# Attention of a small vision tower: values held still and turned probabilities streamed, instead of the other way round

## The reference, cut to what matters

```python
q, k, v = ...                                  # (64, 16, 37, 16), q and k rotated
scores = einsum('bhtd,bhsd->bhts', q, k) / sqrt(16)
probs = softmax(scores, axis=-1)
attn = einsum('bhts,bhsd->bhtd', probs, v)
attn = attn.transpose(0, 2, 1, 3).reshape(B, T, C)
h = h + attn @ Wout + bout
```

## Time and profile before

| | us |
|---|---|
| median of three executions | 336.23 |
| the profiled execution | 335.01 |
| its span in the trace | 333.2 |
| PE busy in the span | 304.5 (91%) |
| DVE busy | 254.3 (76%) |
| ACT busy | 195.0 (59%) |
| POOL busy | 138.9 (42%) |

### The profile page before, as it was taken

One profiled execution on the slowest core, in us unless ns is written; L12 is line 12 of the kernel. 1 busy time (PEld: TensorE's weight loads), 2 busy tenths in 40 slices (PEclk: granted clock), 3 DMA queues, 4 the chain that ended last, 5 costly groups with the idle time before them and its releaser, 6 DMA issues.

```text
span 333.2 us, 9403 instructions
## 1 busy us (share of the span) xinstructions
PE 304.5 (91%) x3575; PEld 232.7 (70%) x3583; DVE 254.3 (76%) x666; ACT 195.0 (59%) x366; POOL 138.9 (42%) x262
## 2 busy tenths in 40 slices
PE   8989899999999977998999999999768999999784
PEld 8877676777777644656877777877645777776552
DVE  1778996677757774356888877887489999999982
ACT  0323433545544335447655666655548999999992
POOL 0356665645654467437900000000065565666520
PEclk9999999999999999999999999999999999999996
DMA  6799560010000100113211121111000001000011
GB/s 227 230 369 401 165 223 17 18 36 17 19 17 17 36 17 17 51 35 79 54 42 44 40 47 45 40 47 29 3 0 0 3 32 34 31 33 31 33 48 55
DMA packets 19307, 22.38 MB, mean 67 GB/s; under 512 B 2304, under 2 KB 15888, under 8 KB 19264
## 3 DMA queue, kind: packets, MB, share of 16 engines
q1 hardware_dynamic: 18544, 20.89, 19.3%
q10 hardware_dynamic: 720, 0.90, 1.0%
HBM read 16.76 MB, written 5.02 MB: 65 GB/s over the span
## 4 chain that ended last, share of the span: by engine, by line
PE 68%; DVE 18%; ACT 8%; issue 4%; POOL 1%; DVEq 0%; ACTq 0%
PE ps L414 15%; PE ps L454 10%; PE ps L528 9%; DVE sc L913 7%; PE ps L551 7%; PE ps L432 5%; DVE ximg L934 4%; PE ps L518 4%; PE ps L402 4%; PE ps L536 3%; ACT ximg L1125 3%; PE ps L462 2%; ACT ximg L1120 2%; PE ps L499 2%; PE ps L393 2%
## 5 line engine op out<-in xcount | busy, mean ns | idle before, releaser
L1159 POOL TENSOR_TENSOR rs<-rs,nhalf 128x1 f32<-128x1 f32 (+1 forms) x76 | 45.4, 597 | 159.2 <-DVE rs L907 101.2
L414 PE MATMUL ps<-w_in,xT 128*128 128x256 f32 (+1 forms) x228 | 52.6, 380 | 0.6 <-ACT xT L992 0.6
L414 PEld LDWEIGHTS ps<-w_in,xT 128*128 128x128 f32 (+1 forms) x228 | 41.2, 187 | 6.5 <-ACT xT L992 0.8
L1077 ACT ACTIVATE ximg<-ps 128x296 f32<-128x296 f32 x64 | 26.6, 418 | 30.0 <-PE ps L528 29.4
L998 ACT ACTIVATE hn<-h,nmr,rs 128x256 f32<-128x256 f32 (+1 forms) x19 | 11.4, 600 | 54.9 <-POOL nmr L1179 54.9
L454 PE MATMUL ps<-w_qk,hnT 128*128 128x512 f32 (+1 forms) x76 | 36.2, 598 | 3.5 <-DVE qb L793 3.5
L528 PE MATMUL ps<-tab,ximg 128*128 128x128 f32 x256 | 34.9, 279 | 0.0
L851 DVE TENSOR_REDUCE ximg<-ps 128x16 f32<-128x592 f32 x32 | 24.7, 772 | 13.3 <-PE ps L518 13.1
L1166 POOL TENSOR_TENSOR qa<-qa,qb 128x512 f32<-128x512 f32 (+1 forms) x19 | 24.1, 1266 | 13.0 <-DVE qb L793 13.0
L528 PEld LDWEIGHTS ps<-tab,ximg 128*128 128x128 f32 x256 | 27.4, 141 | 1.3
L714 DVE SCALAR_TENSOR_TENSOR h<-ymid,rs,ps 128x256 f32<-128x256 f32 (+1 forms) x19 | 9.1, 480 | 24.8 <-PE ps L393 20.4
(11 more groups left out here) (110 smaller groups left out, 666.6 us busy)
## 6 DMA issues: line engine op xcount, KB each, us to landing
ximg<-in_x SPq DMA_DIRECT2D x18, 384.0 KB, 10.3
ximg<-vsc SPq DMA_DIRECT2D x64, 51.0 KB, 1.9
vsc<-vt SPq DMA_DIRECT2D x18, 136.0 KB, 1.7
out<-ximg SPq DMA_DIRECT2D x18, 128.0 KB, 1.7
ximg<-in_W SPq DMA_DIRECT2D x2, 1024.0 KB, 6.3
qkT<-in_W SPq DMA_DIRECT2D x2, 384.0 KB, 4.8
wide<-in_rows SPq DMA_DIRECT2D x1, 640.0 KB, 10.5
qkT<-in_offsets ACTq DMA_DIRECT2D x1, 512.0 KB, 4.0
```

Source lines behind the costliest of these rows:

```text
L414: mm = pe.matmul(dst[0:n, :], xT[t % 2][:, k, 0:n], w_in[:, k, :], start=(k == 0), stop=(k == KP - 1))
L1077: act.activation(pT[p % 2][:, g0:g0 + 4, :, :], ps_pT(b), ACT.Copy).then_inc(S[f"p_evac{b}"], 1)
L1159: pool.tensor_tensor(rs[u][0:n, i:i + 1], rs[u][0:n, i:i + 1], nhalf[0:n, :], ALU.pow).then_inc(S[done], 1)
```

## The change

The roles in `attend` are exchanged. A pair of heads' 32 value columns are held still and the turned probabilities of one image (37 columns) stream. The output comes out turned: 32 features on 32 partitions (32c to 32c+31, c = 0 to 3), tokens along the free dimension. The column of ones is gone; instead four matmuls a pair of images hold a block of ones (`head_sum`, 128 x 32: the first 16 columns sum the even head's rows, the last 16 the odd head's) and stream 148 columns each, which gives the sum of each token and head repeated on that head's 16 partitions. `normalise` now takes a reciprocal of 128 x 148 and multiplies 128 x 148 straight into the canvas. `turn_out` and `attended_out` go, with the semaphores o_norm, o_turned and a_init and the two memsets of PSUM on DVE (L880, L884). The value row in `vt`, `vsc` and `vb` grows from 272 to 512 numbers: each head pair takes 32 columns, with zeros where the other head's values would be, set once by POOL.

```diff
-VROW = 2 * HC * VW
+VROW = 2 * D
...
+        head_sum = sb("head_sum", [128, 2, HD])
...
-                    src = bass.AP(vsc.tensor, PW * p * VROW + e * HC * VW,
-                                  [[VROW, 48], [TOK * VROW, 2], [1, HC * VW]])
-                    sp.dma_start(vb[p % 4][64 * e:64 * e + 48, :, e, :], src).then_inc(S[f"vb{p % 4}"], 16)
+                    src = bass.AP(vsc.tensor, PW * p * VROW + e * D,
+                                  [[VROW, 48], [TOK * VROW, 2], [1, D]])
+                    sp.dma_start(vb[p % 4][64 * e:64 * e + 48, :, :], src).then_inc(S[f"vb{p % 4}"], 16)
...
             def attend(p):
                 war(pe, "o_canvas", p)
-                if p < 2:
-                    pe.wait_ge(S["a_init"], p + 1)
+                if p == 0:
+                    pe.wait_ge(S["qk_rot"], NT + 1)
+                if p == 1:
+                    pe.wait_ge(S["qk_canvas"], NT + 1)
                 pe.wait_ge(S["p_evac4"], p + 1)
                 pe.wait_ge(S["p_evac5"], p + 1)
+                for c in range(4):
+                    probs = pT[p % 2][:, :, :, :].rearrange("p (m c) i t -> p c m (i t)", c=4)[:, c, :, :]
+                    pe.matmul(ps_sums(p % 2)[32 * c:32 * c + 32, :, :], head_sum[:, :, :].rearrange("p e c -> p (e c)"), probs, start=True, stop=True)
                 pe.wait_ge(S[f"vb{p % 4}"], 32 * (p // 4 + 1))
-                for g in range(HC):
+                for m in range(2):
                     for i in range(2):
-                        rhs = vb[p % 4][:, i, :, VW * g:VW * g + VW]
-                        dst = ps[64 * i:64 * i + TOK, 6 + p % 2, 2 * VW * g:2 * VW * g + 2 * VW]
-                        mm = pe.matmul(dst.rearrange("p (e c) -> p e c", e=2), pT[p % 2][:, g, i, :], rhs,
-                                       start=True, stop=True)
+                        for c in range(4):
+                            g = 4 * m + c
+                            mm = pe.matmul(ps_out(p % 2)[32 * c:32 * c + 32, m, TOK * i:TOK * i + TOK],
+                                           vb[p % 4][:, i, 2 * HD * g:2 * HD * g + 2 * HD], pT[p % 2][:, g, i, :],
+                                           start=True, stop=True)
                 mm.then_inc(S["o_ready"], 1)
...
-                if live(s - 3, NP):
-                    turn_out(s - 3)
...
+            for e in range(2):
+                for c in range(2):
+                    v.memset(head_sum[64 * e:64 * e + 64, c, :], 1.0 if c == e else 0.0)
...
             def normalise(p):
                 u = p % 2
                 v.wait_ge(S["o_ready"], p + 1)
-                v.reciprocal(rec[u][0:SPAN, :].unsqueeze(2), ps_o(u)[:, :, HD:VW]).then_inc(S["o_rec"], 1)
+                v.reciprocal(rec[u], ps_sums(u)).then_inc(S["o_rec"], 1)
                 v.wait_ge(S["o_rec"], p + 1)
-                war(v, "o_turned", p, 4)
-                v.tensor_tensor(at[p % 4][0:SPAN, :].rearrange("p (h c) -> p h c", c=HD), ps_o(u)[:, :, 0:HD],
-                                rec[u][0:SPAN, :].unsqueeze(2).to_broadcast([SPAN, NH, HD]), ALU.mult
-                                ).then_inc(S["o_norm"], 1)
+                v.tensor_tensor(qkT[:, 0:2, PW * p:PW * p + PW], ps_out(u), rec[u], ALU.mult
+                                ).then_inc(S["o_canvas"], 1)
...
-            v.memset(ps[:, 6, 0:NH * VW], 1.0).then_inc(S["a_init"], 1)
...
-            v.memset(ps[:, 7, 0:NH * VW], 1.0).then_inc(S["a_init"], 1)
...
-                if live(s - 3, NP):
-                    attended_out(s - 3)
...
-                        ins = pool.memset(vt[u][:, :, :, :], 1.0)
-                    ins.then_inc(S["v_ones"], 1)
+                        ins = pool.memset(vt[u][:, :, :, :, :], 0.0)
+                    ins.then_inc(S["v_blank"], 1)
```

More of the change, by code:

```diff
@@ L33 @@
 K3 = 3 * TOK
-SPAN = 64 + TOK
 V3 = 3 * TOK
-VW = HD + 1
 HC = NH // 2
-VROW = 2 * HC * VW
+VROW = 2 * D
 LAG = 9
@@ L177, in vit_block @@
         later = carve(pix[:, GPX:NT * PD], 2 * [
-            ([NH, 64], F32), ([HC, 2, TOK], F32), ([NH], F32), ([NH], F32), ([2, 128], BF16), ([D], F32)]
-            + 4 * [([D], F32)] + 4 * [([2, 2, HC * VW], F32)])
+            ([NH, 64], F32), ([HC, 2, TOK], F32), ([NH], F32), ([2, PW], F32), ([2, 128], BF16), ([D], F32)]
+            + 4 * [([2, D], F32)])
         pr, pT, mx, rec, nT, ob = zip(later[:6], later[6:12])
-        at, vb = later[12:16], later[16:20]
+        vb = later[12:16]
         ps = ctx.enter_context(nc.psum_tensor("ps", [128, 8, 512], F32))
@@ L194, in vit_block @@
             "w_abs w_tot w_sc w_rc w_q w_done "
-            "orow v_ready v_evac v_ones v_stored0 v_stored1 v_zero p_zero vb0 vb1 vb2 vb3 "
-            "a_init s_ready s_max s_sub s_exp p_turned4 p_turned5 p_evac4 p_evac5 "
-            "o_ready o_rec o_norm o_turned o_canvas "
+            "orow v_ready v_evac v_blank v_stored0 v_stored1 v_zero p_zero vb0 vb1 vb2 vb3 "
+            "s_ready s_max s_sub s_exp p_turned4 p_turned5 p_evac4 p_evac5 "
+            "o_ready o_rec o_canvas "
             "m_set z_ready r_sum r_stat r_aggr r_var r_rstd r_nmr r_norm r_amax r_xs r_rc r_dsc r_rnd r_bias n_turned "
@@ L225, in vit_block @@
         hnT = [sb(f"hnT{u}", [128, 2, 128]) for u in range(HB)]
-        vt = two("vt", [128, 2, HC, VW])
+        vt = two("vt", [128, 2, HC, 2, HD])
         hn = two("hn", [128, D])
@@ L269, in vit_block, with ps_out, ps_sums @@
         ps_w = ps[:, 2, D:D + 2]
-        O_AT = NH * VW
         def ps_pT(b):
             return bass.AP(ps, 512 * b, [[4096, 128], [128, 4], [64, 2], [1, TOK]])
[L275 to L279, removed]
+        def ps_out(u):
+            return ps[:, 6 + u, 0:2 * PW].rearrange("p (m c) -> p m c", m=2)
+        def ps_sums(u):
+            return ps[:, 6 + u, 2 * PW:4 * PW].rearrange("p (m c) -> p m c", m=2)
         def tiles_of(p):
@@ L326, in store_values @@
                 sp.wait_ge(S["v_evac"], t + 1)
-                sp.dma_start(vsc[128 * t:128 * t + n, :], vt[t % 2][0:n, :, :, :].rearrange("p e g c -> p (e g c)")
+                sp.dma_start(vsc[128 * t:128 * t + n, :], vt[t % 2][0:n, :, :, :, :].rearrange("p e g a c -> p (e g a c)")
                              ).then_inc(S[f"v_stored{t % 2}"], 16)
@@ L878, in _ @@
             patch_step(NT + LAG + 1)
-            v.wait_ge(S["qk_rot"], NT + 1)
-            v.memset(ps[:, 6, 0:NH * VW], 1.0).then_inc(S["a_init"], 1)
             attention_step(1)
             attention_step(2)
-            v.wait_ge(S["qk_canvas"], NT + 1)
-            v.memset(ps[:, 7, 0:NH * VW], 1.0).then_inc(S["a_init"], 1)
             for s in range(3, NP + 3):
@@ L1010, in values_out @@
                 if t < 2:
-                    act.wait_ge(S["v_ones"], 1)
+                    act.wait_ge(S["v_blank"], 1)
                 else:
@@ L1014, in values_out @@
                 n = rows(t)
-                act.activation(vt[t % 2][0:n, :, :, 0:HD],
+                act.activation(bass.AP(vt[t % 2], 0, [[VROW, n], [D + HD, 2], [2 * HD, HC], [1, HD]]),
                                ps_v[0:n, :].rearrange("p (g e d) -> p e g d", e=2, d=HD), ACT.Copy
@@ L1065, in _ @@
                     act.activation(w2t[:, :, :], w2[:, :, :], ACT.Abs, accum_out=wabs[:, 1:2]).then_inc(S["w_abs"], 1)
[L1067 to L1071, removed]
             def probs_out(p, b):
@@ L1216, in _ @@
             for u in range(4):
-                pool.memset(vb[u][:, :, :, :], 0.0).then_inc(S["v_zero"], 1)
+                pool.memset(vb[u][:, :, :], 0.0).then_inc(S["v_zero"], 1)
                 patch_step(NT + 3 + u)
```

## The result

The changed kernel took 340.44 us (median of 11 executions, 338.84 to 341.44), the kernel before 336.23 us (median of 11, 335.27 to 338.11). Ratios leave out slow executions, as 594.69 us (rows widened, first time), 508.97 us (one-column matmuls) and 336.90 us (logarithms on ScalarE). The changed kernel is slower by 1.2%, as forecast (341, range 334 to 347).

The account below looks back on a forecast made before the run. PE bounded the kernel before, DVE close behind; DVE would take over. 28 x (2.81 - 2.65) = +4.5, entrance +0.4, exit -0.3: +4.6 us, median 340.8, say 341; range 336 to 345, stretched to 334 to 347.

Parts of the forecast that it names:

- The reciprocal sets the step: DVE in attention: reciprocal of 148 elements takes 1.04 us, DVE step 2.81 us above PE's 2.21; 28 steps cost +4.5 us.
- the quick reciprocal: Rival, DVE normalise: excess is fixed cost, reciprocal 0.40 us, PE sets the step at 2.36, 327 us; chance 0.09.
- Stride charged at nothing: DVE's old reciprocal reads sums 17 words apart in PSUM; this explains none of its time, so no cost was charged.
- eight passes: Rival, DVE normalise: 8.4 ns an element, reciprocal 1.39 us, step 3.16, 351 us; chance 0.04.
- PE's issue stops fall there too, so I add none: PE in attention: its stops for "issue" fall under normalise's 1.3 us while scores waits, adding nothing to the 2.81 us step.
- Column tiles four abreast: PE's new attend: four column tiles overlap 3.1 of 4, 0.76 us; rival of less overlap, 350 or 373 us, chance 0.05.
- Entrance and exit: Ends of attention: first reciprocal delays maximum 3 by +0.4 us; after the last maximum the residual comes earlier, -0.3 us.
- Elsewhere nothing: Outside the step: larger stores and loads and POOL's longer memset of vt were taken to cost 0 us.

Follow-up runs that it names:

- rows widened, first time: Kernel before with only the value rows widened as in the change (512 numbers stored, 256 a load; nothing reads the added ones): ratio 1.0042.
- one-column matmuls: Changed kernel with 16 matmuls of one bf16 column added to each call of attend, 32 more instructions a step, nothing reads them: 348.23 us, ratio 1.0333.
- logarithms on ScalarE: Changed kernel with reciprocals made on ScalarE as exp(-ln(sum)) and half of attend ahead of a wait, whole computation: 334.35 us, ratio 0.9955.
- the prices: Kernel before with reciprocals of several sizes and a multiplication appended to DVE, pow and multiplication to POOL: the 148-element reciprocal 1.02 us, 6.26 ns an element.
- sums thrice: Changed kernel with the four matmuls of sums issued three times over, same results: 367.98 us, ratio 1.0946.
- wide matmul: Changed kernel with one float32 matmul of 128 rows, 128 x 200 columns, added to each attend, 4 more instructions: 342.75 us, ratio 1.0219.
- no sums either: Changed kernel with the reciprocal replaced by a multiplication and the matmuls of sums left out from the third pair on: 330.73 us, ratio 0.9867.
- no reciprocal: Changed kernel with its 128x148 reciprocal replaced by a multiplication by one, division by the sums left out: 335.38 us, ratio 0.9971.

## Why the prediction was right

- **The reciprocal sets the step: right, and nearly in size.** 1.04 us forecast, 1.07 measured; 6.0 ns an element taken, 6.26 measured. The step from 1 to 16 elements between rows of the kernel before pointed the right way, but it was a thin base: back to back the prices have 158 ns for one and 196 for 16, which would have given 2.5 ns an element and spoken for the quick reciprocal; the 6.26 show from 16 elements up (196, 558, 1021). So the size owes something to luck. DVE's clean step came to 2.83 us against 2.81, and with the reciprocal replaced by a multiplication the mean step falls to 2.68 and the time by 5 us.
- **Stride charged at nothing, eight passes rejected: right,** shown by the prices, with the reserve on the stride said there.
- **"PE's issue stops fall there too, so I add none": wrong in size.** The mean step is 2.89, not 2.83: 28 x 0.06 = 1.7 us. A stop is covered only while PE would wait anyway; the one ahead of the row at 163.58 falls into the middle of scores, and the next maximum starts 2.98 us behind the last (160.88 to 163.86) instead of 2.83. Between the two traces the spans differ by 6.2 us: 6.7 in the 28 steps where 4.5 were forecast (0.6 from the clean step, 1.7 from the stops), +0.1 up to maximum 3, -0.4 at the exit, -0.2 behind it. The medians differ by only 4.2.
- **The agreement to 0.4 us (340.8 against 340.44) is partly luck.** The steps of the trace cost 2.2 us more than forecast, and that the profiled executions lie 1.2 below and 0.9 above their medians takes about as much off again. The mechanism does not hang on it.
- **Column tiles four abreast: right, and a little better.** 0.69 us for attend where 0.76 was taken: 2.37 us alone, so 3.4 abreast. The run with three matmuls a tile in a row shows that this hangs on the order of the stream.
- **Entrance and exit.** +0.4 forecast: L851 of pair 2 starts at 156.03 and the maximum of pair 3 at 158.06, 2.03 us behind it, against 1.60 from L855, the same subtraction before: +0.43. But pair 2 came 0.37 us earlier than before, which I had not counted on, so maximum 3 starts only 0.06 later. -0.3 forecast: the residual starts 6.78 us behind the last maximum against 7.14, -0.36.
- **Elsewhere nothing:** not contradicted, but not shown to better than 1.6 us; the widened rows alone gave 1.0042 and 1.0016.
- **The quick-reciprocal rival was priced wrongly.** I gave it 327 us by leaving PE's stops at their 0.15 us a step. The run without a reciprocal took 335.4, so the relief of PE was worth about 1 us here, 2 at most by the interval. The failing step is the sentence that PE would set the step with 2.21 + 0.15: the mean step without the reciprocal is 2.68, of which 0.36 lie above the shortest, and the loop turn_probs, copy, attend adds 0.18 to the shortest.

What the change did, then: it took 0.36 us of clean work a step off PE, of which little could be cashed in, and put 0.70 us more on DVE (2.83 against 2.13: 0.82 for the reciprocal, less 0.11 for the shorter multiplication), which had 0.52 to spare. The 0.18 left over are the step from 2.65 to the clean 2.83.

That the stops belong to the arrival of instructions is inferred from where they lie, behind the 16 KB transfers, and from the pair of runs with the same work in 4 and in 32 instructions. What sets their length is open: no run changed the size or the timing of a transfer. By stage, with instructions a step as the code issues them:

| kernel | instructions a step | shortest step | the same a us | mean step | mean above shortest | records a us |
|---|---|---|---|---|---|---|
| sums thrice | 192 | 3.65 | 53 | 3.66 | 0.01 | 52.6 |
| change | 160 | 2.82 | 57 | 2.89 | 0.07 | 55.6 |
| wide matmul | 164 | 2.82 | 58 | 2.89 | 0.07 | 56.7 |
| before | 148 | 2.48 | 60 | 2.65 | 0.17 | 55.9 |
| no sums either | 144 | 2.32 | 62 | 2.56 | 0.24 | 56.9 |
| tiny matmuls | 192 | 2.82 | 68 | 3.09 | 0.27 | 61.7 |
| no reciprocal | 160 | 2.32 | 69 | 2.68 | 0.36 | 59.3 |
| logarithms on ScalarE | 160 | 2.32 | 69 | 2.63 | 0.31 | 61.2 |

The third column of numbers is instructions a step over the shortest step: how fast PE uses instructions when nothing stops it. The gap between the shortest and the mean step grows with it. (In the row of the wide matmul the gap is the regular step of 2.89; it has no stops.) No kernel passed 62 records a microsecond over a whole stage, though single steps ran at 68 and 69. A fixed time a block does not fit: 256 instructions last 4.6 us in the change and 4.5 in the kernel without sums, and both have stops, while with logarithms on ScalarE 256 pass in 4.2.

## What to carry to other kernels

Price an operation by its slope between two sizes in the trace, better between large ones than small ones, and not by one row: a reciprocal of 16 elements looked like a quarter of a microsecond of overhead, but behind it stood six times the usual cost per element. Turning a layout moves every per-token quantity to one value per element, so count what the elementwise engine gets in exchange for the matmul engine's relief. And where PE runs many small matmuls, count its instructions as a resource of their own: in these runs the stops for issue cost the more, the less work stood between the instructions.

## What the hardware showed that I had not expected

- PE's instructions seem to come in the 16 KB transfers, 3.2 to 5.8 us apart in attention; all 96 stops for "issue" end 2.2 to 3.0 us behind one. Over the stage the stream did not exceed 62 records a microsecond, and less other DMA traffic (6 GB/s instead of 81) left the step at 2.63 us.
- Behind a stop of 1.45 us PE's granted clock fell to 0.56 to 0.59 of full speed for about 4 us, in the run with one-column matmuls only; in the traces of the other versions of the change, with stops of up to 0.95 us, it stayed at 1.00 throughout attention.
- Matmuls on four column tiles overlap less when the tile changes seldom: 24 records of 148 columns took about 1.6 us in blocks of six a tile, while 8 in rotation took 0.28.
- ScalarE takes a logarithm and an exponential of 128x148 in 0.28 and 0.33 us without a table load between them.
- POOL's pow takes 2.9 us for 16 elements a partition, about 0.55 for one.
